# First layer of an expert loop in three chunks of 64 features, in two row groups of TensorE

## What is computed

```python
xf = x.reshape(-1, D)                                   # 1024 tokens, D = 192
combine = gw[:, :, None] * ew                           # 4 groups x 8 experts; 2 groups and 4 experts of each are kept
for g in range(G):
    h = gelu(einsum('nd,edm->enm', xf, W1[g]) + b1[g][:, None, :])   # M = 768 hidden features
    o = einsum('enm,emd->end', h, W2[g]) + b2[g][:, None, :]
    y = y + einsum('end,ne->nd', o, combine[:, g, :])
```

## Time and profile before

| | |
|---|---|
| runs | 757.8, 754.62, 754.21 us; median 754.62 us |
| profiled execution | 753.57 us, of which the span from first to last instruction is 751.8 us |
| PE busy | 678.0 us, 90% of the span |
| DVE, ACT, POOL busy | 406.3, 239.4, 305.6 us |
| mean granted clock of PE | 0.919 |

### The profile page before, as it was taken

The page is one execution under the profiler, slowest core; times in us unless marked ns, Lnnn a source line. Parts: engine busy times, 40 slices in busy tenths (PEclk is TensorE's granted clock), DMA queues, the critical chain, the costliest instruction groups (busy, mean ns, idle before and its releaser), DMA issues.

```text
span 751.8 us, 20437 instructions
## 1 busy us (share of the span) xinstructions
PE 678.0 (90%) x6550; PEld 573.0 (76%) x6550; DVE 406.3 (54%) x1222; ACT 239.4 (32%) x686; POOL 305.6 (41%) x288
## 2 busy tenths in 40 slices
PE   6986959898989999857699999999999999999994
PEld 4753746656655688754698899999999999999994
DVE  6636483755378778878733444444444444444442
ACT  3321312123227511113343333333333333333331
POOL 0012830011022555411335565555655555655654
PEclk9996968667999999985599999999999999999998
DMA  8910000000000001232238654465546566465422
GB/s 316 279 38 2 2 3 2 3 1 3 1 1 0 1 2 48 81 126 82 51 93 236 171 162 121 113 172 114 136 114 189 129 170 174 113 173 133 91 46 39
DMA packets 36136, 70.07 MB, mean 93 GB/s; under 512 B 6481, under 2 KB 21362, under 8 KB 36082
## 3 DMA queue, kind: packets, MB, share of 16 engines
q0 software_dynamic: 15840, 17.71, 13.8%
q10 hardware_dynamic: 8064, 33.12, 13.0%
q1 hardware_dynamic: 12178, 18.48, 7.8%
HBM read 59.31 MB, written 9.98 MB: 92 GB/s over the span
## 4 chain that ended last, share of the span: by engine, by line
PE 59%; DVE 18%; DMA 11%; issue 6%; SPq 3%; POOL 2%; ACT 1%; POOLq 0%; DVEq 0%; ACTq 0%
PE bank L1618 16%; PE bank L1610 11%; PE bank L1613 7%; DMA out_dram<-arena,number_u 5%; DMA arena<-normed_rows,fetch_u 4%; PE bank L1436 4%; PE bank L1368 4%; PE bank L1590 3%; PE bank L1388 2%; DVE stats L942 2%; DVE zx L956 2%; PE bank L1379 1%; PE bank L1406 1%; DVE arena L1176 1%; DVE arena L1173 1%
## 5 line engine op out<-in xcount | busy, mean ns | idle before, releaser
L654 POOL DMA_INDIRECT out_dram<-arena,number_u x80 | 126.8, 1585 | 50.1 <-DMA out_dram<-arena,number_u 22.6
L648 POOL DMA_INDIRECT arena<-normed_rows,fetch_u x80 | 78.5, 982 | 113.3 <-DMA out_dram<-arena,number_u 52.5
L841 ACT ACTIVATE arena<-bank,arena 128x128 f32<-128x128 f32 x234 | 64.6, 375 | 113.0 <-PE bank L1613 113.0
L1260 DVE COPY arena<-bank 128x256 f32<-128x256 f32 x81 | 34.4, 425 | 110.5 <-PE bank L1590 101.9
L1618 PE MATMUL bank<-arena 128*128 128x192 f32 x468 | 82.7, 326 | 0.0
L1618 PEld LDWEIGHTS bank<-arena 128*128 128x128 f32 x468 | 75.4, 190 | 0.0
L1279 DVE TENSOR_SCALAR arena<-bank,arena 128x192 f32 x80 | 33.4, 418 | 59.8 <-PE bank L1618 58.2
L551 POOL TENSOR_SCALAR rstd<-mv 128x4 f32<-128x4 f32 (+1 forms) x15 | 3.6, 237 | 142.3 <-DVE mv L945 142.3
L1610 PE MATMUL bank<-arena 128*128 128x128 f32 x468 | 58.7, 275 | 0.4 <-DVE arena L1260 0.4
L841 ACT ACTIVATE arena<-bank,w_space 128x128 f32<-128x128 f32 x132 | 36.4, 375 | 68.6 <-PE bank L1613 68.6
L1610 PEld LDWEIGHTS bank<-arena 128*128 128x128 f32 x468 | 57.2, 192 | 0.9 <-DVE arena L1260 0.9
(11 more groups left out here) (259 smaller groups left out, 1239.2 us busy)
## 6 DMA issues: line engine op xcount, KB each, us to landing
arena<-in_moe_w_dram ACTq DMA_DIRECT2D x14, 579.0 KB, 5.7
arena<-in_moe_w_dram ACTq DMA_DIRECT2D x14, 576.0 KB, 4.1
arena<-in_xf_dram SPq DMA_DIRECT2D x16, 256.0 KB, 10.4
w_space<-in_moe_w_dram ACTq DMA_DIRECT2D x7, 579.0 KB, 5.4
w2small<-in_moe_w_dram ACTq DMA_DIRECT2D x7, 579.0 KB
w_space<-in_moe_w_dram ACTq DMA_DIRECT2D x7, 576.0 KB, 3.9
wab<-in_moe_w_dram ACTq DMA_DIRECT2D x7, 576.0 KB
arena<-in_w_dram SPq DMA_DIRECT2D x8, 480.0 KB, 7.9
```

What stands on the lines that cost most here:

```text
L648: pool.indirect_dma_start(out=mo_stage[:, s * ROWN:(s + 1) * ROWN], out_offset=None, in_=normed_rows, in_offset=bass.IndirectOffsetOnAxis( ...
L654: pool.indirect_dma_start(out=out, out_offset=bass.IndirectOffsetOnAxis(ap=number_u[:, s:s + 1], axis=0), in_=mo_res[:, s * D:(s + 1) * D] ...
L841: nc.scalar.activation(mo_hT[:, m, :], bank[2 + m][:, 0:P], ACT.Gelu, bias=b1[:, m:m + 1]).then_inc(free[2 + m], 1)
L1260: nc.vector.tensor_copy(mo_xT.rearrange("p k t -> p (k t)"), bank[1][:, 0:2 * P]).then_inc(free[1], 1)
```

## The change

The features are cut into three chunks of 64. Each chunk now stands twice in `mo_x`, so that each of three transposes puts it into both halves of the partitions. All of the first layer is done on 64 rows of the array at a time: for three blocks of outputs, and in each for the three chunks, one matmul in rows 0 to 63 (hidden block n) and one in rows 64 to 127 (hidden block n + 3). The gelus and the second layer take the hidden blocks in the order in which they are finished: 0, 3, 1, 4, 2, 5. The weights of the first layer are laid out for it on the host; their number is the same. One product of the table ahead of the loop goes to another bank.

```diff
+CHUNKS = D // 64
+HIDDEN_DONE = tuple(m + half for m in range(MC // 2) for half in (0, MC // 2))
-W1N = HID + MC // 2 * P
+W1N = MC // 2 * CHUNKS * P
...
-        mo_x = view(P, 2 * P)
-        mo_xT = view(P, 2 * P).rearrange("p (k t) -> p k t", k=2)
+        mo_x = view(P, CHUNKS * P)
+        mo_xT = view(P, CHUNKS * P).rearrange("p (k t) -> p k t", k=CHUNKS)
...
-                use(5, "table", 1)
+                use(7, "table", 1)
...
-                    for m in range(MC):
+                    for m in HIDDEN_DONE:
                         act.wait_ge(full[2 + m], i + (moe_base[2 + m] + 1))
                         nc.scalar.activation(mo_hT[:, m, :], bank[2 + m][:, 0:P], ACT.Gelu, bias=b1[:, m:m + 1]).then_inc(free[2 + m], 1)
...
-                nc.vector.tensor_copy(mo_x[:, D:2 * P], mo_stage[:, bass.ds(i % STAGE * ROWN + P, REST)])
-                nc.vector.tensor_copy(mo_x[:, 0:D], mo_stage[:, bass.ds(i % STAGE * ROWN, D)]).then_inc(sem("rows_staged"), 1)
+                for half in range(2):
+                    ins = nc.vector.tensor_copy(mo_x.rearrange("p (k h x) -> p k h x", k=CHUNKS, h=2)[:, :, half, :], mo_stage[:, bass.ds(i % STAGE * ROWN, D)].rearrange("p (k x) -> p k x", k=CHUNKS))
+                ins.then_inc(sem("rows_staged"), 1)
...
-                nc.vector.tensor_copy(mo_xT.rearrange("p k t -> p (k t)"), bank[1][:, 0:2 * P]).then_inc(free[1], 1)
+                nc.vector.tensor_copy(mo_xT.rearrange("p k t -> p (k t)"), bank[1][:, 0:CHUNKS * P]).then_inc(free[1], 1)
...
-                for k in range(2):
+                for k in range(CHUNKS):
                     ins = nc.tensor.transpose(bank[1][:, k * P:(k + 1) * P], mo_x[:, k * P:(k + 1) * P], ident[:])
...
-                    for m in range(MC):
-                        mm(bank[2 + m][:, 0:P], w1e[:, m * P:(m + 1) * P], mo_xT[:, 0, :], start=True, stop=False)
-                    for m in range(MC):
-                        r, c = m % 2 * REST, HID + m // 2 * P
-                        mm(bank[2 + m][:, 0:P], w1e[r:r + REST, c:c + P], mo_xT[r:r + REST, 1, :], start=False, stop=True).then_inc(full[2 + m], 1)
+                    for n in range(MC // 2):
+                        for k in range(CHUNKS):
+                            c = (n * CHUNKS + k) * P
+                            for r, m in ((0, n), (REST, n + MC // 2)):
+                                ins = mm(bank[2 + m][:, 0:P], w1e[r:r + REST, c:c + P], mo_xT[r:r + REST, k, :], start=(k == 0), stop=(k == CHUNKS - 1))
+                                if k == CHUNKS - 1:
+                                    ins.then_inc(full[2 + m], 1)
...
-                    for m in range(MC):
+                    for n, m in enumerate(HIDDEN_DONE):
                         pe.wait_ge(free[2 + m], i + (moe_base[2 + m] + 1))
-                        ins = mm(bank[0][:, 0:D], mo_hT[:, m, :], w2e[:, m, :], start=(m == 0), stop=(m == MC - 1))
+                        ins = mm(bank[0][:, 0:D], mo_hT[:, m, :], w2e[:, m, :], start=(n == 0), stop=(n == MC - 1))
...
-        "moe_w1": np.concatenate([i["L1_ffn_W1"].reshape(NE, D, HID)[:, :P],
-                                  i["L1_ffn_W1"].reshape(NE, D, HID)[:, P:].reshape(NE, REST, MC // 2, 2, P).transpose(0, 3, 1, 2, 4).reshape(NE, P, MC // 2 * P)], 2),
+        "moe_w1": i["L1_ffn_W1"].reshape(NE, CHUNKS, REST, 2, MC // 2, P).transpose(0, 3, 2, 4, 1, 5).reshape(NE, P, W1N),
```

## The result

The changed kernel took 766.15 us (median of 4 runs, 760.31 to 770.77) against 754.41 us for the kernel before: a ratio of 1.0127, 95% interval 1.0082 to 1.0173. Forecast were 763.3 us, in a range of 758 to 768; the median lies in it, two of the four runs (768.09 and 770.77) lie above it. The profiled execution took 764.22 us, 10.65 us more than that of before.

A forecast was written before the change was run, and what follows sets the result against it. PE's own sequence was taken to bound the expert loop. Third transpose 8.8, start 0.4 and first layer 0.0 made +9.2 us, giving 762.8 from the profiled execution and 763.8 from the median; forecast 763.3 us, range 758 to 768.

The forecast's parts named there:

- Third transpose, 8.8 us: On PE ahead of the second layer: 0.11 us more per tile, nothing to hide it, 8.8 us over 80 tiles.
- First layer, 18 steps against 18, difference 0: PE's first layer per tile: 12 full passes and 6 pairs become 18 pairs, 2.30 us before and after.
- the lower bound: First layer on PE: a step of 0.109 us, which L1473's train of pairs comes near to, would save 4.3 us.
- Switches: PE between full array and halves: two per tile before and after, some 0.09 us each beyond a step.
- DVE: L1260 reads 384 columns instead of 256, 0.57 us; DVE gets 0.2 us more per tile, hidden in usual tiles.
- The two staging copies: On DVE: both become the wider kind, 0.29 + 0.29 us against 0.23 + 0.29, hidden in usual tiles.
- PE's waits, taken as 0: PE's waits in the first layer for L1260: change taken as 0, bounds -2.9 to +0.6 us.
- The start, +0.4: Loop's start, nothing hides DVE: +0.15 for L1260, +0.06 for copies, some 0.2 for a third transpose.
- Pairs that hide loads better: Rival in L1616: cheaper steps than full passes; at 0.108 us and four waits gone, 755.4 us; chance 10%.
- Loss of concurrency or of the clock in steady tiles: Rival on PE: pairs run one after the other, 923 us, or half-array work lowers the clock, 880 us; 4%.
- A longer DVE round: Rival: DVE's round grows until PE waits in many tiles; 0.1 us in all tiles would be 771 us; 4%.
- The rule of the Trainium skill: On PE's weight loads: full-array steps would carry open loads, paired ones not, so the change would win; leads to the 10% rival.

The follow-up runs named there:

- e1: Changed kernel with two transposes per tile instead of three and the copy back at 256 columns: 755.27 us, 1.0033 of the kernel before.
- e2: Kernel before with a third transpose per tile that nobody reads: 761.13 us, 1.0136 of the kernel before.
- e7: Changed kernel with one idle transpose per tile ahead of the other three: 768.82 us, 1.0238 of the kernel before.
- e3: Changed kernel with one idle transpose per tile between the first and second block of outputs: 796.87 us (one run).
- e6: Kernel before with DVE's copy of the transposed rows widened from 256 to 384 columns: 756.27 us, 1.0011 of the kernel before.
- e4: Changed kernel with the weight loads inside the expert loop cut to 128 columns of each matrix: 758.66 us.
- e5: Kernel before with the weight loads inside the expert loop cut to 128 columns of each matrix: 749.48 us.

## Why the prediction was right

- **Third transpose, 8.8 us: right.** Steady tiles went from 4.53 to 4.64 us, 8.8 us over 79 periods. Undone, the loss goes (e1); put alone into the kernel before, the loss comes (e2); a further one costs 0.10 us per tile again (e7). Transposes to second layer took 0.39 us, as the forecast said they would.
- **First layer, 18 steps against 18, difference 0: right.** Steps of 0.112, an open load of 0.101 and switches as read off. e1 has all of the new first layer at the old period. One reading behind the lower bound was off: L1473 has weights of 128 rows and 64 columns, so its pairs halve the array's columns, not its rows, and say nothing sure of L1616. The sum did not use it.
- **Switches: right.** The number is unchanged and so is the price; e3 paid 0.46 us per tile for an added pair of them with its transpose, where the rows of before gave 0.45.
- **DVE: right.** 0.558 us against 0.57, hidden (e6). The two staging copies took 0.35 us each on average where I had 0.29; hidden too.
- **PE's waits, taken as 0: mis-sized.** The long tiles grew by 2.2 us in the profiled pair, and the bounds I gave were -2.9 to +0.6. PE stood 1.5 us longer (4.4 against 2.9), and beside the standing these tiles lost 1.74 us against 1.05. The train and the transposes behind the first stop, partly at the lower clock, took 1.36 us longer by themselves; a clock that falls behind a stop was not in the term. The reading of where they come from (POOL's adds, L1286, L1263) was right. That the weight loads are behind it was in no row I used; e4 and e5 show it. In the runs the term is not clear of noise: against 9.2 us without any waits, the changed kernel lost 11.7 us by its first four runs and 9.8 by the ten later ones. Whether the change itself lengthens the waits stays open: e2, e3 and e7, with a PE as slow or slower, waited 0.9, 0 and 1.1 us in their one profile each, the changed kernel 4.4 and 6.0 in two, all from 376 us on.
- **The start, +0.4: seen in part, and made up for.** PE's first wait for the copied rows grew from 0.59 to 0.72 us (forecast +0.15), and from the first transposes to the first layer were 1.25 us in place of 1.00. But the first tile as a whole took 5.07 us against 4.96: 0.11 more, which is the third transpose that the 8.8 us already hold. In the sum, 0.4 us that did not come thus hid a little of what the waits were short by; that part is luck. When the loop starts says nothing of it: in the profiled executions its first transposes began between 371.1 and 375.5 us. PE's first work of the first layer, before and after:

```profile
373.89 2.44 PE L1610 MATMUL bank<-arena,w_space 128*128 128x128 f32 x12 [0.59 <-DVE arena L1260]
```

```profile
373.59 3.89 PE L1616 MATMUL bank<-arena,w_space 64*128 64x128 f32 x36 [0.72 <-DVE arena L1263]
```

- **The rivals.** Pairs that hide loads better (10%): out, a pair is 0.112 in a train of 18 too. Loss of concurrency or of the clock in steady tiles: out. A longer DVE round: out by e6. The rule of the Trainium skill (TensorE: Matmul & The Clock Gate, "The mechanism") that only another row group's loads overlap with matmuls in flight doesn't hold here: loads of the whole array took 0.192 us each beside passes that start every 0.111 us, and with the pairs in two row groups a step is no shorter, 0.112. The same section also has loads into a background weight buffer pulled ahead of matmuls; no run here shows that buffer, but these rows don't conflict with it.

## What to carry to other kernels

Where an engine is busy all the time, count its steps before and after and take their price from starts in the trace: this rearrangement kept the number of steps and of switches and gained nothing, and what it needed in addition, one transpose per tile, was paid in full. Two half-array matmuls side by side took as long as one full one (0.112 us against 0.111); they pay for a contraction that would leave half of the array empty, not for one that fills it. A wait that an engine inherits through three others is worth tracing to the transfer behind it before more buffers are built: if the program that waits for the late transfer does so before it issues the next fetch, the wait only moves.

## What the runs showed of the hardware that I had not expected

- A stop of PE of 1.43 us left the next train at 2.28 us, stops of 2.12 and 3.85 us made it 3.33 and 3.81 us; but in the same execution as the 2.12 one, a stop of 2.29 us at 432.39 was followed by a train of 2.28. The stretches with these stops (410 to 435 us, and 420 to 445 when repeated) have a granted clock of 0.93, their neighbours 1.00. In the kernel before, whose longest stop in the loop was 1.39 us, it is 1.00 from 400 to 440 us.
